# Attention tiles of every fourth query row, and a stored matrix read in 2 KB pieces

## The reference

```python
scores = einsum('bhqd,bhkd->bhqk', q, k)
pos_emb = dist_emb[pos_l - pos_r + 255]          # 512 x 512 x 16
rel_q = einsum('bhld,lrd->bhlr', q, pos_emb)
rel_k = einsum('bhrd,lrd->bhlr', k, pos_emb)
scores = (scores + rel_q + rel_k) / 4
probs = softmax(scores); ctx = einsum('bhqk,bhkd->bhqd', probs, v)
```

## Time and profile before

| | |
|---|---|
| median of 3 runs | 3637.33 us (3631.33 to 3641.29) |
| profiled execution: time, span | 3640.87 us, 3639.3 us |
| busy share of the span | TensorE matmul 76%, VectorE 63%, ScalarE 49%, GpSimd 22% |
| DMA of the whole program | 848.79 MB in 899306 packets, mean 233 GB/s |
| first load of R issued, last tile of `add` | 1606.1 us, 2864.8 us |

### The profile page before, as it was taken

One profiled execution on the slowest core, in us unless ns is written; L12 is line 12 of the kernel. 1 busy time (PEld: TensorE's weight loads), 2 busy tenths in 40 slices (PEclk: granted clock), 3 DMA queues, 4 the chain that ended last, 5 costly groups with the idle time before them and its releaser, 6 DMA issues. The chain is left out here.

```text
span 3639.3 us, 69041 instructions
## 1 busy us (share of the span) xinstructions
PE 2756.1 (76%) x18124; PEld 1921.6 (53%) x18124; DVE 2294.1 (63%) x6133; ACT 1772.2 (49%) x3509; POOL 807.3 (22%) x907
## 2 busy tenths in 40 slices
PE   4665676776767767638878888878888688888887
PEld 2443576665766767635545555545555344444443
DVE  5664354554545545438877888878888666666664
ACT  2443453443534445318877888878888511111111
POOL 2442110111111111001211222212121224433334
PEclk7888575666766667659888999989999889999999
DMA  4999898979889799899999999999999711111110
GB/s 114 226 221 209 183 358 314 340 289 334 330 312 365 291 345 338 325 292 279 264 254 268 270 274 273 267 257 275 274 276 274 212 43 61 61 61 61 61 61 19
DMA packets 899306, 848.79 MB, mean 233 GB/s; under 512 B 236808, under 2 KB 809536, under 8 KB 864688
## 3 DMA queue, kind: packets, MB, share of 16 engines
q1 hardware_dynamic: 840112, 640.95, 60.2%
q0 software_dynamic: 59136, 207.14, 21.0%
HBM read 507.88 MB, written 340.05 MB: 233 GB/s over the span
## 5 line engine op out<-in xcount | busy, mean ns | idle before, releaser
L697 DVE TENSOR_TENSOR d_r<-d_pk,d_r 128x1024 f32<-128x1024 f32 x512 | 620.9, 1224 | 622.1 <-PE d_pk L654 487.9
L684 ACT ACTIVATE d_r<-d_pq 128x1024 f32<-128x1024 f32 x512 | 532.6, 1052 | 693.4 <-PE d_pq L643 686.9
L1035 ACT ACTIVATE t_e<-t_neg,t_low 128x512 f32<-128x512 f32 x1024 | 738.7, 734 | 231.5 <-DVE t_low L977 230.1
L643 PE MATMUL d_pq<-d_win,d_q 96*128 96x128 bf16 x4096 | 488.1, 278 | 303.1 <-DMA d_q<-q_chunks_scratch 283.4
L977 DVE CUSTOM_DVE_ANT_0 t_neg<-t_ps,t_r 128x512 f32<-128x512 f32 x1024 | 671.8, 687 | 28.4 <-issue 28.3
L903 PE MATMUL t_pt<-t_ident,t_e 128*128 128x128 f32 x4096 | 642.0, 280 | 1.5 <-DVE t_eT L985 0.6
L643 PEld LDWEIGHTS d_pq<-d_win,d_q 96*128 96x128 bf16 x4096 | 433.5, 193 | 327.8 <-issue 229.6
L893 PE MATMUL t_ps<-t_kb,t_qa 96*128 (+1 forms) x1024 | 405.0, 396 | 247.6 <-DVE t_low L977 182.5
L903 PEld LDWEIGHTS t_pt<-t_ident,t_e 128*128 128x128 f32 x4096 | 518.0, 145 | 110.9 <-ACT t_eT L1042 13.7
L654 PE MATMUL d_pk<-d_win,d_k 96*128 96x128 bf16 x4096 | 501.5, 288 | 76.6 <-DMA d_k<-k_chunks_scratch 45.1
L654 PEld LDWEIGHTS d_pk<-d_win,d_k 96*128 96x128 bf16 x4096 | 441.1, 187 | 105.0 <-DVE d_r L697 56.7
(11 more groups left out here) (133 smaller groups left out, 2560.3 us busy)
## 6 DMA issues: line engine op xcount, KB each, us to landing
r_scratch<-d_r SPq DMA_DIRECT2D x256, 1024.0 KB, 18.4
t_r<-r_scratch SPq DMA_DIRECT2D x1024, 256.0 KB, 5.3
d_q<-q_chunks_scratch POOLq DMA_DIRECT2D x64, 768.0 KB, 16.0
d_q<-q_chunks_scratch POOLq DMA_DIRECT2D x64, 512.0 KB, 17.8
d_q<-q_chunks_scratch POOLq DMA_DIRECT2D x64, 256.0 KB, 19.6
t_kb<-k_chunks_scratch POOLq DMA_DIRECT2D x32, 512.0 KB, 20.3
q_chunks_scratch<-a_part SPq DMA_DIRECT2D x96, 128.0 KB, 3.6
q_rows_scratch<-a_part SPq DMA_DIRECT2D x96, 128.0 KB, 2.2
```

What stands on the lines that cost most here:

```text
L643: last = nc.tensor.matmul(pq[n % 2][:, a, :], q[u][:, :, l % CW], rhs, start=True, stop=True)
L684: nc.scalar.activation(r[u][:, n * QL:(n + 1) * QL, :], pq[n % 2][:], ACT.Copy).then_inc(q_out, 1)
L697: nc.vector.tensor_tensor(part, pk[n % 2][:].rearrange("p r l -> p l r"), part, ALU.add).then_inc(k_added, 1)
L1035: nc.scalar.activation(e[:, j % 2, L, :], neg[:, L, :], ACT.Exp, bias=low[:, j % 2, L:L + 1], scale=-1.0, accum_out=total[:, j // GH, L, j ...
```

## The change

The four tiles of a head no longer hold 128 neighbouring query rows each. Partition p of tile t now holds query row 4p + t. With that, partition p needs the four neighbouring query rows 4p to 4p + 3, which lie together in `r_d` as 2 KB for each key chunk. The loads of R change to match: for each head four DMAs, one for each chunk lc of 128 query rows, each of 256 KB to the 32 partitions 32 lc to 32 lc + 31, in pieces of 2 KB. A head has one semaphore, VectorE waits for it once, before the head's first tile, and SyncE waits until all four tiles of the head four earlier are used. The weights of the score matmul are read with a step of four elements, the R operand of `add` with its key chunks 2 KB apart, and `scale` writes its result with a step of four elements to bring the query rows back into order.

```diff
-        r = sb("t_r", [P, RR, TT, NT, TB])
+        r = sb("t_r", [P, RR, NT, TT, TB])
-        r_loaded = [sem(f"t_r_loaded{i}") for i in range(RR * TT)]
+        r_loaded = [sem(f"t_r_loaded{i}") for i in range(RR)]
+        HEAD = 16 * NT
                 def load_r(g, n, j):
-                    for L in range(TT):
-                        later(sp, added, TT * (n - RR) + L + 1)
-                        sp.dma_start(r[:, j % RR, L], r_d[g][L, :, n - g * P, 0:TB * TB].rearrange("c (l r) -> l c r", r=TB)
-                                     ).then_inc(r_loaded[j % RR * TT + L], 16)
+                    later(sp, added, TT * (n - RR + 1))
+                    for lc in range(NT):
+                        src = r_d[g][lc, :, n - g * P, 0:TB * TB].rearrange("c (p x) -> p c x", x=TT * TB)
+                        sp.dma_start(r[lc * P // NT:(lc + 1) * P // NT, j % RR].rearrange("p c t r -> p c (t r)"), src
+                                     ).then_inc(r_loaded[j % RR], 16)
                 def score(n, j, L, slot):
-                    nc.tensor.matmul(p_s[bank(j, L)][:], qa[:, 0, slot, L * P:(L + 1) * P], kb[:, :, slot, :],
+                    nc.tensor.matmul(p_s[bank(j, L)][:], qa[:, 0, slot, :].rearrange("r (p t) -> r t p", t=TT)[:, L, :], kb[:, :, slot, :],
                 def add(n, j, L, loads):
-                    dve.wait_ge(r_loaded[j % RR * TT + L], 16 * loads)
+                    if L == 0:
+                        dve.wait_ge(r_loaded[j % RR], HEAD * loads)
-                    nc.vector.tensor_tensor_reduce(out=neg[:, L, :], in0=p_s[bank(j, L)][:], in1=r[:, j % RR, L].rearrange("p c r -> p (c r)"), scale=-0.25,
+                    nc.vector.tensor_tensor_reduce(out=neg[:, L, :].rearrange("p (c r) -> p c r", r=TB),
+                                                   in0=p_s[bank(j, L)][:].rearrange("p (c r) -> p c r", r=TB),
+                                                   in1=r[:, j % RR, :, L, :], scale=-0.25,
                 def scale(G, par, stores):
-                    nc.vector.tensor_tensor(out[:, par, :], p_c[:], wideT[:], ALU.mult).then_inc(ctx_done, 1)
+                    nc.vector.tensor_tensor(out[:, par, :].rearrange("c (p t) -> c t p", t=TT),
+                                            p_c[:].rearrange("c (t p) -> c t p", t=TT),
+                                            wideT[:].rearrange("c (t p) -> c t p", t=TT), ALU.mult).then_inc(ctx_done, 1)
```

## The result

| | before | after |
|---|---|---|
| median, us | 3634.62 (4 runs) | 3878.51 (4 runs, 3859.41 to 3894.79) |
| profiled execution, us | 3640.87 | 3894.79 |
| first load of R issued to last tile of `add`, us | 1258.7 | 1508.2 (1614.0 to 3122.2) |

The ratio of after to before is 1.0667, with a 95% interval of 1.0614 to 1.0719: slower by 6.7%. The forecast was 3890, and 1510 us for the attention.

A forecast was written before the change was run, and what follows sets the result against it. DMA work was taken to bound the attention: R and v 1208 us plus batch loads 299 make 1507 against 1259, +248, and +3 for waits, giving 3890 us after rounding; own range 3790 to 4060, 8-in-10 range 3640 to 4060.

The forecast's parts named there:

- a serial sum of DMA work: Attention before: 1024 loads of R with v at 0.909 us plus 16 batch loads of 20.5 us make 1259 us.
- The step from t_kb's landings to R: New loads of R: 1.15 us for 256 KB, taken from t_kb's landings at 32 partitions; ends 0.63 and 1.3.
- the three DMAs that it averaged: Batch load: 512 KB DMAs to 32 partitions took 2.1, 2.6 and 2.2 us; mean 2.3, so 1.15 for 256 KB.
- Half of what R gains lengthens the load: Batch load: R's larger packets gain up to 3.5 us a load; half taken, 20.5 - 1.8 = 18.7 us.
- The forecast for the waits: VectorE's wait for a whole head of R: only the last head pays, up to three tiles, +3 us.
- the cover named: VectorE: a doubled L998 costs 44 us, under the slower loads' cover of 0.7 us a head, 179 us.
- L998 at 681 ns: Sign of being right, in `scale`: its multiply L998 stays unchanged at 681 ns despite the strided write.
- the allowed 100: Score's strided weight loads on TensorE: between 0 and 0.1 us more a tile, hidden.
- its coarser wait costs nothing, since it hardly waits: SyncE's queue: waiting for a whole used head costs nothing, as it waited only 19.2 us for the buffer before.
- No overlap across the halves: DMAs to alternate partition halves: t_kb's pair took 2.6 + 2.2 us, so the new R loads don't overlap.
- faster: Rival, chance 0.18: packets decide R's loads, up to 0.63 us a DMA; engines bound, -145 us, 3496 us.
- part overlap: Rival, chance 0.09: R's DMAs partly overlap, 0.85 to 1.03 us each; +44 us, 3685 us.

The follow-up runs named there:

- o_before_spread: Kernel before with the batch load of q and k in four portions, TensorE's wait for it moved, v one head later: 3680.74 us, ratio 1.0133.
- j_before_early: Kernel before with the batch load of q and k issued before the widening of the next group's sums: 3638.76 us, ratio 0.9996.
- g_after_small: Kernel after, but from the third batch on a batch load brings q and k of the first head alone, in the same seven DMAs: 3635.56 us.
- c_32part_512B: Kernel before with the coarser waits and each head's R as four 256 KB DMAs to 32 partitions in 512-byte pieces: 3939.23 us, ratio 1.0815.
- e_64part: Kernel d_128part, but each of a head's four R DMAs writes 64 partitions, lower half twice, then upper half twice: 3877.99 us, ratio 1.0647.
- a_waits: Kernel before with only the coarser waits, one semaphore a head; R loads unchanged: 3653.54 us, ratio 1.0039.
- f_order: Kernel after with a head's four R DMAs in the order 0, 64, 32, 96 of first partition: 3789.99 us, ratio 1.0386.
- d_128part: Kernel after with R stored so that a head's four 256 KB DMAs, one a key chunk, write 128 partitions in 2 KB pieces: 3643.00 us, ratio 1.0010.

## Why the prediction was right

- The bound. That the attention before is a serial sum of DMA work, and not a wait for late q and k, is borne out by o_before_spread (no gain, and DMA engines as busy); j_before_early (no change) excludes only the late q and k. The sum isn't exact: it has no term for the 49 us of o_before_spread.
- The step from t_kb's landings to R. 1.15 us for 256 KB to 32 partitions, with v 1.18; g_after_small measures 1.184. That the partitions set it and not the pieces is shown by c_32part_512B, that it is the half and not their number by e_64part. The prediction read the number of partitions out of its rows and had the half from the Trainium skill; its rows couldn't tell them apart, since one of the three DMAs that it averaged, to partitions 48 to 79, reaches into both halves.
- Luck in the number. The pace was not steady: one load of R in 1.25 us from 2000 to 2040 us, in 1.05 (38 in 40 us) from 2935 to 2975, and periods from 100.3 down to 89.2 us. The forecast, which knows only one pace, met their mean. And the 1.15 was read while packets of R took 10.0% of the engines' time beside t_kb's, which the prediction didn't take off.
- The range. By its own terms (1.05 to 1.3 us, both ends of the batch load) it goes from some 3760 to 4070, not from 3790 to 4060. The result is in both.
- The batch load: 18.7 us each in the sum, 17.4 by g_after_small's time and 19.3 by its period. "Half of what R gains lengthens the load" was a choice between ends and fell near the middle.
- The forecast for the waits was 3 us at the end; alone they cost some 14 (a_waits). In after they may be hidden by the slower stream; the attention came out 2 us under its sum.
- `scale`: taken unchanged with a doubling as the end; it grew by 62%, 64 x 0.42 = 27 us, under the cover named, and its sign "L998 at 681 ns" failed. The weights grew by 15 ns of the allowed 100.
- SyncE: "its coarser wait costs nothing, since it hardly waits" was wrong as a reason. It came to wait 299.5 us for the buffer. c_32part_512B, which hardly waits and is no faster, makes it unlikely that the waits set the pace; taking them out of after was not tried.
- "No overlap across the halves" was too strong. One pair in the trace (2.6 + 2.2 us) bore it; f_order shows a part of it, and e_64part's start a phase with much more. The drift of after's pace may be the same thing; that was not shown. The rivals "faster" and "part overlap" were nearer than this one pair made them look.
- The rival "faster" had its own fault, which d_128part lays open: it let a four-head buffer cover 20.5 us of batch load but for 0 to 5 us. The stall was 14.1 us. Had R come as fast as in d_128part, the time would have been near 3640, not 3496.

## What to carry to other kernels

Read the speed of a planned transfer off one in the trace that writes the same partitions, not off one with the same bytes: a stream of DMAs into one half of the partitions each ran at some 230 GB/s in quiet stretches, whether a DMA wrote 32 or 64 of them (with phases up to 291), the same stream into all 128 at up to 375. To get larger pieces, change how the data lies in memory, so that one DMA still spans all partitions. And a stream that has become fast enough helps only when the bursts beside it are shorter than its buffer: the layout gained nothing until the batch load was cut up.

## What the runs showed of the hardware that was not expected

- VectorE's multiply of 512 columns took 1100 ns when it wrote with a step of four float32 elements and 681 without; reading R with 2 KB steps between its chunks cost `add` nothing (689 and 687 ns).
- 2 KB packets of R to 128 partitions ran at 375 GB/s in a stretch of 5 us, with a DMA share of 1.04; at 512 bytes it was 290 with a share of 1.20.
- Beside a batch load two queues got nearly equal numbers of packets, whatever the packets' size: 552 against 532 with 2 KB, 344 against 358 with 512 bytes.
- TensorE's clock stayed at 1.00 over 55 us with TensorE busy 48.82 us, with many short pauses, and was 0.50 in the long stalls.
